# One round of variances for two chained norms, and fewer root chains in a stack's run-out

## What is computed

```python
x = x + 0.5 * ffn_stack(layernorm(x))                # six layers
x = x + attn_block(layernorm(x))                     # the middle block
x = x + 0.5 * ffn_stack(layernorm(x))                # the same six layers again
```

```python
h = layernorm(x)                                     # eps 1e-5, no gain
y = layernorm(h) * norm1_g + norm1_b                 # eps 1e-5
h = h + proj(linear_attention(y)) ; x = x + h + mlp(layernorm(h) * norm2_g + norm2_b)
```

## Time and profile before

| | us |
|---|---|
| median of three runs | 3810.95 (3795.51 to 3813.49) |
| profiled execution | 3810.15 |
| its span | 3808.1 |
| TensorE busy | 3549.3 (93%) |
| VectorE busy | 2853.6 (75%) |
| GpSimd busy | 2731.1 (72%) |
| ScalarE busy | 2486.6 (65%) |

### The profile page before, as it was taken

How to read it: one execution, slowest core, us unless ns; L and a number is a source line. 1 busy time by engine, 2 the same in 40 slices (tenths; PEclk the granted TensorE clock), 3 DMA queues, 4 the chain that set the end, 5 groups by cost and what they waited for, 6 DMA issues and landing times.

```text
span 3808.1 us, 152943 instructions
## 1 busy us (share of the span) xinstructions
PE 3549.3 (93%) x64080; PEld 2726.9 (72%) x64080; DVE 2853.6 (75%) x5172; ACT 2486.6 (65%) x3088; POOL 2731.1 (72%) x2152
## 2 busy tenths in 40 slices
PE   6999999999999999998677999999999999999996
PEld 4777777777777777776335777777777777777773
DVE  4778778777878777786446877778777787778774
ACT  4677666776777777674225767767766767766762
POOL 5877777887787787874006877777787787787770
PEclk8999999999999999998788999999999999999997
DMA  3232232332232232231002322323322332322220
GB/s 91 76 80 76 74 80 76 77 83 73 77 84 75 74 86 71 74 87 51 6 0 63 82 77 75 84 73 77 85 74 75 81 81 76 84 76 70 71 65 23
DMA packets 207418, 272.71 MB, mean 72 GB/s; under 512 B 55700, under 2 KB 101648, under 8 KB 206736
## 3 DMA queue, kind: packets, MB, share of 16 engines
q1 hardware_dynamic: 206736, 262.94, 26.7%
HBM read 60.35 MB, written 1.05 MB: 16 GB/s over the span
## 4 chain that ended last, share of the span: by engine, by line
PE 40%; issue 5%; DVE 3%; ACT 2%; POOL 1%; DVEq 1%; POOLq 0%; ACTq 0%
PE PS L328 8%; PE PS L431 5%; PE PS L376 4%; PE PS L461 4%; PE PS L495 3%; PE PS L378 3%; PE PS L377 3%; PE PS L504 2%; PE PS L530 2%; PE PS L424 1%; POOL V L1189 1%; PE PS L545 1%; PE PS L516 1%; ACT PR L739 1%; PE PS L313 1%
## 5 line engine op out<-in xcount | busy, mean ns | idle before, releaser
L1189 POOL TENSOR_TENSOR V<-RAWQK,TAB 128x512 f32<-128x512 f32 x768 | 964.9, 1279 | 625.0 <-PE PS L328 608.8
L376 PE MATMUL PS<-WH,XH 128*128 128x512 f32 x1152 | 525.1, 456 | 34.3 <-POOL XL L1169 29.9
L1215 POOL TENSOR_TENSOR V<-V,U 128x1024 f32<-128x1024 f32 x192 | 454.3, 2366 | 29.0 <-POOL V L1189 2.2
L377 PE MATMUL PS<-WH,XL 128*128 128x512 f32 x1152 | 470.1, 408 | 1.5 <-issue 1.5
L378 PE MATMUL PS<-WL,XH 128*128 128x512 f32 x1152 | 471.1, 409 | 0.0
L1231 POOL TENSOR_TENSOR V<-V,U 128x1024 f32<-128x1024 f32 x192 | 454.9, 2369 | 15.2
L431 PEld LDWEIGHTS PS<-KT,QT 64*32 64x32 f32 x24576 | 366.5, 107 | 132.7 <-issue 132.4
L461 PEld LDWEIGHTS PS<-V,PT 64*32 64x32 f32 x24576 | 342.1, 107 | 160.8 <-issue 156.3
L431 PE MATMUL PS<-KT,QT 64*32 64x64 f32 x24576 | 436.4, 218 | 17.5 <-issue 16.3
L328 PEld LDWEIGHTS PS<-EYE,V 128*128 128x128 f32 x3072 | 349.0, 141 | 118.4 <-issue 115.8
L461 PE MATMUL PS<-V,PT 64*32 64x64 f32 x24576 | 382.9, 219 | 45.8 <-issue 44.1
(11 more groups left out here) (151 smaller groups left out, 7346.5 us busy)
## 6 DMA issues: line engine op xcount, KB each, us to landing
V<-VS SPq DMA_DIRECT2D x3072, 64.0 KB, 2.0
ROTB<-c_rot SPq DMA_DIRECT2D x192, 128.0 KB, 2.5
WSTAGE<-wqkv SPq DMA_DIRECT2D x33, 512.0 KB, 3.9
WO<-wo SPq DMA_DIRECT2D x12, 512.0 KB, 3.8
W<-w SPq DMA_DIRECT2D x12, 341.0 KB, 3.4
QKS<-qks SPq DMA_DIRECT2D x12, 128.0 KB, 3.6
W<-w SPq DMA_DIRECT2D x12, 114.0 KB
VS<-wqkv SPq DMA_DIRECT2D x2, 512.0 KB, 4.2
```

What stands on the lines that cost most here:

```text
L376: pe.matmul(o, XH[:, p, :], WH[:, w, cols], start=True, stop=False)
L377: pe.matmul(o, XL[:, p, :], WH[:, w, cols], start=False, stop=False)
L1189: ins = pool.tensor_tensor(paired(V[:, k])[:, :, :, h * half:(h + 1) * half], split(RAWQK[:, k])[:, :, :, (1 - h) * half:(2 - h) * half], ...
L1215: pool.tensor_tensor(V[:, 0], V[:, 0], U[:, 0], ALU.add).then_inc(q_turned, 1)
```

## The change

Part one: `norm(c)` returns for chunks that neither exist nor carry a group's variances. `chain_count` counts by place in the list of the remaining chains, `CHAIN_AT` (chunks 0 to 95 and 99); chain 99 waits in addition for the diagonals of the group before. Part two: at the start of the middle block the variances v of x are formed once. With r = 1/sqrt(v + eps), the variance of the normed values is v r r, so the second norm's factor on the centred x is r / sqrt(v r r + eps). VectorE computes both factors, makes two sets of diagonals, TensorE spreads both (the second into banks 3 and 4), and VectorE writes XB and XNM from the same centred values. The centring, squares and variances of call b = 2 go on all engines; later calls are numbered one lower. The key and value products of group 0 wait for `m_ln` at 8.

```diff
+        def normed_group(c):
+            q, g = phase(c + 1 - CHAIN_OFF)
+            return g if q == 1 and 0 <= g < NGR else None
+        CHAIN_AT = [c for c in range(CHAINS) if live(c) or normed_group(c) is not None]
         def chain_count(inv, c):
-            return inv * CHAINS + c + 1
+            return inv * len(CHAIN_AT) + CHAIN_AT.index(c) + 1
...
                 def norm(c):
-                    if not 0 <= c < CHAINS:
+                    if c not in CHAIN_AT:
                         return
...
+                    if not live(c):
+                        held(diag_done, group_count(inv, normed_group(c) - 1))
...
-                    pe.matmul(PS[:, 5 + n % 2, :], SPREAD[:, :], DIAGM[:, n % 2, :], start=True, stop=True).then_inc(m_rb, 1)
+                    mm = pe.matmul(PS[:, 5 + n % 2, :], SPREAD[:, :], DIAGM[:, n % 2, :], start=True, stop=True)
+                    if twice:
+                        mm = pe.matmul(PS[:, 3 + n % 2, :], SPREAD[:, :], D2M[:, n % 2, :], start=True, stop=True)
+                    mm.then_inc(m_rb, 1)
...
-            norm_all(1, lambda g: group(XR, g), xr_half, [1, 2, 3, 4])
-            norm_all(2, lambda g: group(XB, g, 1), m_ln, [5, 6, 7, 8])
+            norm_all(1, lambda g: group(XR, g), xr_half, [1, 2, 3, 4], twice=True)
...
                 if g > 0:
                     sum_kv(g - 1)
+                pe.wait_ge(m_ln, 8)
                 for j in range(4):
                     mm = pe.matmul(PS[:, 3 + j // 2, (j % 2) * 256:(j % 2 + 1) * 256], XNM[:, g, j * P:(j + 1) * P],
...
+            def norm_twice(b, first, second, gain, bias):
+                dve.wait_ge(m_var, 4 * b + 4)
+                dve.tensor_copy(SSM[:, :], PS[:, VAR, 0:16])
+                dve.tensor_copy(SUM[:, 0, :], PS[:, VAR, 0:16])
+                dve.drain()
+                r, rr = RN[:, 0, 0:HEADS], RN[:, 1, 0:HEADS]
+                rsqrt([(r, slice(0, HEADS))], SSM[:, :], NY[:, 0:HEADS], NU[:, 0:HEADS], NV[:, 0:HEADS], EPS, ALU.add).then_inc(m_r, 1)
+                dve.drain()
+                dve.scalar_tensor_tensor(SSM[:, :], SUM[:, 0, :], RSQRT_UNIT * RSQRT_UNIT, r, ALU.mult, ALU.mult)
+                dve.drain()
+                dve.tensor_tensor(SSM[:, :], SSM[:, :], r, ALU.mult)
+                dve.drain()
+                rsqrt([(rr, slice(0, HEADS))], SSM[:, :], NY[:, 0:HEADS], NU[:, 0:HEADS], NV[:, 0:HEADS], EPS, ALU.add)
+                dve.drain()
+                dve.scalar_tensor_tensor(rr, rr, RSQRT_UNIT, r, ALU.mult, ALU.mult)
+                dve.drain()
+                def apply(g):
+                    n = 4 * b + g
+                    dve.wait_ge(m_rb, n + 1)
+                    dve.wait_ge(m_dg, n + 1)
+                    dve.tensor_tensor(second(g), DG4[:, g, :], PS[:, 3 + n % 2, :], ALU.mult)
+                    dve.tensor_tensor(first(g), DG4[:, g, :], PS[:, 5 + n % 2, :], ALU.mult)
+                    dve.drain()
+                    dve.tensor_scalar(second(g), second(g), gain, bias, ALU.mult, ALU.add).then_inc(m_ln, 1)
+                for g in range(NG):
+                    n = 4 * b + g
+                    if g >= 2:
+                        dve.wait_ge(m_rb, n - 1)
+                    for j in range(4):
+                        d = slice(j * P, (j + 1) * P)
+                        dve.tensor_scalar(DIAGM[:, n % 2, d], EYE[:, :], r[:, 4 * g + j:4 * g + j + 1], None, ALU.mult)
+                        ins = dve.tensor_scalar(D2M[:, n % 2, d], EYE[:, :], rr[:, 4 * g + j:4 * g + j + 1], None, ALU.mult)
+                    ins.then_inc(m_diag, 1)
+                    if g > 0:
+                        apply(g - 1)
+                apply(NG - 1)
...
-            norm_all(1, lambda g: group(XB, g, 1))
-            norm_all(2, lambda g: XNM[:, g, :], MSMALL[:, M_B1:M_B1 + 1])
+            norm_twice(1, lambda g: group(XB, g, 1), lambda g: XNM[:, g, :], MSMALL[:, M_G1:M_G1 + 1], MSMALL[:, M_B1:M_B1 + 1])
```

More of the change, by code:

```diff
@@ L57 @@
 B_F3 = 1
-LAG, CHAIN_OFF, CHAINS = 7, 0, 106
+LAG, SEED_LAG, CHAIN_OFF, CHAINS = 7, 0, 0, 106
 B_NORM = 7
@@ L295, in _, with norm_all @@
                     mm.then_inc(xt_ready, 1)
-            def norm_all(b, rhs, ready, values):
+            def norm_all(b, rhs, ready, values, twice=False):
                 def variance(g):
@@ L585, in sum_kv @@
                 mm.then_inc(kv_ready, 1)
-            pe.wait_ge(m_dg, 12)
+            pe.wait_ge(m_dg, 8)
             for g in range(NG):
-                pe.wait_ge(m_ln, 9 + g)
+                pe.wait_ge(m_ln, 5 + g)
                 if g >= 2:
@@ L615, in _ @@
             project_out(NG - 1)
-            norm_all(3, lambda g: group(XB, g, 1), x1_ready, [NG] * NG)
+            norm_all(2, lambda g: group(XB, g, 1), x1_ready, [NG] * NG)
             def fc2(g):
@@ L624, in fc2 @@
                 mm.then_inc(my_ready, 1)
-            pe.wait_ge(m_ln, 16)
+            pe.wait_ge(m_ln, 12)
             for g in range(NG):
@@ L634, in _ @@
             fc2(NG - 1)
-            norm_all(4, lambda g: group(XR, g), xr_mid, [NG] * NG)
+            norm_all(3, lambda g: group(XR, g), xr_mid, [NG] * NG)
             stack(1)
@@ L840, in _ @@
             norm_all(1, 1.0)
-            norm_all(2, MSMALL[:, M_G1:M_G1 + 1])
             for g in range(NG):
@@ L852, in _ @@
                 act.activation(EL[:, a + 1, :], EL[:, a + 1, :], ACT.Exp).then_inc(ex_k, 1)
-            norm_all(3, MSMALL[:, M_G2:M_G2 + 1])
+            norm_all(2, MSMALL[:, M_G2:M_G2 + 1])
             for g in range(NG):
@@ L860, in _ @@
                                    bias=MSMALL[:, M_FC1B + n:M_FC1B + n + 1]).then_inc(mg_ready, 1)
-            norm_all(4, 1.0)
+            norm_all(3, 1.0)
             stack(1)
@@ L1129, in _ @@
             add_projected(NG - 1)
-            norm_all(3, lambda g: XNM[:, g, :], MSMALL[:, M_B2:M_B2 + 1])
+            norm_all(2, lambda g: XNM[:, g, :], MSMALL[:, M_B2:M_B2 + 1])
             for g in range(NG):
@@ L1136, in _ @@
                 dve.tensor_tensor(group(XR, g), group(XR, g), x, ALU.add).then_inc(xr_mid, 1)
-            norm_all(4, lambda g: group(XA, g, 1), done=xa_done)
+            norm_all(3, lambda g: group(XA, g, 1), done=xa_done)
             stack(1)
```

## The result

The changed kernel took 3765.28 us in the median of six runs (3758.95 to 3777.69), the kernel before 3809.62 in the six runs beside it. The ratio is 0.9903 with a 95% interval of 0.9883 to 0.9923, or 37 us less (29 to 45); the two medians by themselves lie 44 us apart. Run twice more later, against other runs of the kernel before, it gave 0.9894 (0.9865 to 0.9924) and 0.9911 (0.9886 to 0.9937). The forecast was 3776, in a range from 3762 to 3794, so the median lies near the range's low end. The profiled execution took 3765.29 us with a span of 3763.4, 44.7 less than the span of before.

A forecast was written before the change was run, and what follows sets the result against it. TensorE, busy 93% of the span, bounds the kernel, so gains come where it stands still: 10.3 + 10.6 (run-outs) + 6.9 (fused norms) + 5.6 (first norm's clock) + 0.6 (end) = 34.0 us off 3810.15, giving 3776, range 3762 to 3794.

The forecast's parts named there:

- The three steps behind chains: Run-outs: L1009, L1003 and first L1077 start earlier by 1.6, 2.8, 5.9 us in stack one, 1.6, 3.2, 5.9 in two.
- The covered chains: Run-outs: chains 96, 97, 100 and 101 cost nothing, since VectorE waits for TensorE there anyway.
- the bound of 2.6: Each run-out, GpSimd's diagonals to last L530: starting earlier can cost or save 2.6 us through the granted clock; taken as 0.
- the chains were covered: Rival, run-outs: other waits replace those ahead of L1009 and L1003, only 5.9 + 5.9 stay; 3791 us, chance 0.08.
- The clock at the first norm: First norm's variance round: shorter TensorE pause keeps the clock up, 8.2 us instead of 13.82; 5.6 us saved, bounds 0 and 6.5.
- The fused norms: Middle block: copy of variances to second norm's end 22.2 us instead of 29.8; net 6.9 us saved, between 3.4 and 8.6.
- the added wait: Group 0's key and value products wait for the last apply, so L1100 starts 2.7 us after it instead of 2.03: minus 0.7.
- The estimate of 1.1 to 2.0: Fused norms: the fourteen added small VectorE instructions by the skill's fixed cycles, instead of 3.5 us; gain 2 us larger.
- The rival of the lost clock: Fused step's 8.1 us TensorE pause loses the clock at norm 1, spreads, key and value stage, first run-out; 3793 us, chance 0.13.
- The last copies: Kernel end: final transposes at full clock bring the last of four paced copies forward by 1.1 us; 0.6 taken.
- the stacks would stay at 1692 us twice: First to last exponential of each stack: unchanged at 1692 us; moving by more than 5 us would show the forecast wrong.
- slower: Rival, both stacks: an earlier start shifts pauses against the clock; 0.01 less costs some 17 us a stack; 3861 us, chance 0.03.

The follow-up runs named there:

- the kernels with warmed run-outs: Changed kernel plus nine unread matmuls in the fused pause and six per run-out: 3759.04 us; also with four in the stacks' variance-product step: 3758.89 us.
- the second profile of the changed kernel: The changed kernel run again without any edit, against the kernel before: 3765.29 us, ratio 0.9894.
- part one alone: Kernel before with chains 96 to 98 and 100 to 105 left out in both stacks, the two norms as before: 3787.88 us, ratio 0.9953.
- eleven unread matmuls: Kernel before, nothing left out, plus eleven matmuls nobody reads on TensorE between the first stack and the first norm: ratio 0.9986.
- the step of the falls: Changed kernel plus four unread matmuls in the stacks' variance-product step, where the clock mostly falls: ratio 0.9892; in the first-hidden-products step instead: 0.9989, both to the kernel before.

## Why the prediction was right

**The run-outs.** The three steps behind chains were right to 0.1 us in both stacks: 1.6, 2.8 and 5.9 in the first, 1.6, 3.2 and 5.9 in the second. The covered chains were covered. What the forecast took as 0 was the clock: the first run-out lost 2.7 us of its 10.3 (from L1020 to L1014 12.1 instead of 11.1, and from there to the second L540's end 14.4 instead of 12.8), the second won 3.1 beyond its 10.6. That the two nearly cancel is luck. The loss is of the size of the bound of 2.6 and lies where the bound was read, and the kernels with warmed run-outs show that this piece hangs on the clock; but the kernel before has the same 12.0 and 14.5 us in its own second run-out, and the second profile of the changed kernel 11.3 and 12.8 in its first. So either level comes with either kernel. The 3.1 lie ahead of the first step that the change touches, between the last exponential and L545's end, which takes 18.2 to 23.2 us in the profiles at a granted clock between 0.99 and 0.75. The rival "the chains were covered" is out.

**The clock at the first norm.** 6.4 us instead of 5.6: the round took 7.38, by the row at 1.00 and not by the mean of the two rows. That the shorter pause would do it was argued from one row; the kernels with part one alone and with eleven unread matmuls show it, at 8.18 and 8.16 us against 14.6.

**The fused norms.** Copy to the last step 22.7 us against 22.2 in the sum; the added wait cost 2.79 - 2.03 = 0.8 against 0.7. Net 6.3 instead of 6.9. The added small instructions took 3.5 us (first diagonal 6.36 after the copy, 2.90 before), by the row's 0.26. The estimate of 1.1 to 2.0 worked out from the Trainium skill (VectorE: DVE Perf Modes, section "The TRN2 errata") did not hold: there the trace disagrees with the page's table, for dependent instructions with drains between them.

**The rival of the lost clock** was right in one piece: behind the new pause the first four passes did run at half clock, 3.6 us from start to start instead of 1.8. Its price was in the sum already. The rest of it did not happen: the key and value stage stayed at 1.00 from 1852.87 to 1870.00 and fell at the fourth group, as before. Removing one pause paid 6.4 us; adding the other cost 1.8, and the fused step kept its net 6.3 all the same. What the Trainium skill (TensorE: Matmul & The Clock Gate, section "HAM oscillation") says of bursts behind pauses agrees with both: the spreads behind 8.11 us of idle time began at the 1.2 GHz level, the round behind 1.69 did not.

**The last copies.** The last of ScalarE's copies ended 5.6 us behind the first add_half instead of 6.9, so the 1.1 us that the forecast allowed at full clock came in full. But from there to the end it took 4.1 us instead of 3.0, and of the 0.6 taken only 0.2 were left. Why the last part grew is open; over all profiles it takes 3.0 to 4.3 us.

**A mistake in the argument.** The statement that both stacks took the same time within 0.6 us was wrong. The first of the two stretches began one step late (89.19; the first exponential is at 73.53), so it held 94 steps and not 95. Cut alike, the stacks of the kernel before took 1707.63 and 1692.58 us:

```profile
73.53:1781.16 1707.63, 1654.91 (x31417) 1297.83 (x31417) 1336.30 (x2314) 1191.05 (x1469) 1336.22 (x1047) 0.98 0.30 78
```

So the forecast that the stacks would stay at 1692 us twice did not hold (1700.4 and 1690.5), and it had called a movement of over 5 us a sign of error: 7.3 us of the profiled difference lie in the first stack. They lie within the spread that this mistake hid, and no run shows them to be an effect of the change. The rival "slower" had been priced against the same false agreement of the two stacks. The 15 us of chance in a stack were left out of the range's working, which held because the runs' spread had been put in.

**What stays open.** The whole is 37 us by its ratio; the touched stretches give 34. But the two parts timed alone give 18 and 6, 24 together, with intervals of about 6 and 8 us either way. The stretches of part one alone add up to 26, so some 8 us of its stretches' gain are missing from its time, about as much as the stacks differ by chance. In the profile of part one alone the middle block behind L1100 took 4 us longer than before; the changed kernel had 160.5 us there twice and 164.6 once. More executions could tell a rest between the parts from chance; that was not tried.

## What to carry to other kernels

A loop's run-out repeats per-step work for steps that do not exist; on an engine with a low busy share it can stand directly ahead of the only useful work left, so read the timeline there and price only the instances behind which something useful waits (five of nine here). Idle time removed ahead of a burst of matmuls can pay twice, once for itself and once for the burst's clock, as at the first norm here. Before two stretches are called equal, check that they hold the same number of steps.

## What the runs showed of the hardware

- The stacks' length varied by up to 23 us between executions and kernels with the same instructions, and by its time at 1.2 GHz: a stack took 1664 to 1673 us plus half of it.
- Matmuls that nobody reads can cost nothing where they keep the clock up: four of 512 bf16 columns in the step of the falls took no longer than none, the same four two steps later 37 us more.
- TensorE kept 2.4 GHz over an idle time of 1.69 us. Behind the 3.44 us ahead of the final transposes the outcome varied: sixteen took 2.38 us in the first profile of the changed kernel, where the clock fell on the way, and 3.68 in its second, as in the kernel before.
